# First expert stage of a two-layer graph network: logits and mixture turned in whole 128x128 blocks, VectorE and ScalarE work in another order

## The reference, cut to what matters

```python
gp = softmax(xf @ Wr + br)                    # 4 groups of experts
ep = softmax(einsum('nd,gde->nge', xf, Wgate) + bgate)   # 4 experts in each
# of each softmax the best two are kept (ties: lower index first), the second
# only if both together are <= 0.9; then they are normalised to sum 1
tw = w_group[:, :, None] * w_exp * 0.5        # 16 weights for each row
for e in range(16):
    h = silu(xf @ W1[e]) * (xf @ W3[e])       # 512 -> 32
    out = out + tw[:, e:e+1] * (h @ W2[e])    # 32 -> 512
```

## Time and profile before

| | |
|---|---|
| median of 3 runs | 2476.98 us (2475.22 to 2479.04) |
| profiled execution, its own time | 2480.19 us |
| its span in the profile | 2478.5 us |
| PE busy | 2322.9 us (94%) |
| PE weight loads busy | 1847.2 us (75%) |
| VectorE busy | 1789.8 us (72%) |
| ScalarE busy | 1140.3 us (46%) |
| GpSimd busy | 688.3 us (28%) |
| granted TensorE clock, mean | 0.968 of full |

### The profile page before, as it was taken

One profiled execution on the slowest core, in us unless ns is written; L12 is line 12 of the kernel. 1 busy time (PEld: TensorE's weight loads), 2 busy tenths in 40 slices (PEclk: granted clock), 3 DMA queues, 4 the chain that ended last, 5 costly groups with the idle time before them and its releaser, 6 DMA issues. The chain is left out here.

```text
span 2478.5 us, 33401 instructions
## 1 busy us (share of the span) xinstructions
PE 2322.9 (94%) x10767; PEld 1847.2 (75%) x10770; DVE 1789.8 (72%) x4234; ACT 1140.3 (46%) x2096; POOL 688.3 (28%) x624
## 2 busy tenths in 40 slices
PE   6799886999999999999898999999999699999998
PEld 4577665777777777777677878888877577777776
DVE  7587796787877777777565765555556688888886
ACT  6564322435354545454452222222234776766652
POOL 6465023222222212120131221221222533433420
PEclk9899987999999999999999999999999899999999
DMA  5111133121212122220273344333346656656631
GB/s 167 54 52 52 18 128 99 55 98 60 94 65 90 69 85 73 81 83 33 82 232 99 128 138 135 130 130 130 129 139 201 153 138 179 155 150 179 153 102 52
DMA packets 155873, 271.89 MB, mean 110 GB/s; under 512 B 35538, under 2 KB 36178, under 8 KB 155478
## 3 DMA queue, kind: packets, MB, share of 16 engines
q1 hardware_dynamic: 123014, 203.00, 24.4%
q0 software_dynamic: 32720, 67.19, 11.5%
HBM read 185.82 MB, written 100.41 MB: 115 GB/s over the span
## 5 line engine op out<-in xcount | busy, mean ns | idle before, releaser
L2388 ACT ACTIVATE conv_h<-conv_h 128x512 f32<-128x512 f32 x79 | 50.0, 633 | 305.6 <-DVE conv_h L2317 256.7
L2865 POOL DMA_INDIRECT next_own<-message,net_slot_d x75 | 123.5, 1646 | 153.6 <-DMA next_own<-own 136.2
L2286 DVE TENSOR_TENSOR conv_yl<-conv_pty,conv_yh 128x512 fp32r<-128x512 f32 x79 | 54.7, 692 | 150.7 <-ACT conv_yh L2378 141.4
L1732 ACT ACTIVATE d_act_out<-d_pa 128x512 f32<-128x512 f32 (+1 forms) x80 | 46.1, 577 | 200.1 <-PE d_pa L69 200.1
L1023 POOL DMA_INDIRECT early_val<-values,net_slot_s x79 | 85.3, 1080 | 189.7 <-DVE d_x L1501 88.5
L67 PE MATMUL d_po<-shared_wq_hi,d_hh 128*128 128x512 f32 x316 | 130.7, 414 | 7.2 <-DVE d_hl L1507 3.1
L67 PE MATMUL conv_p<-conv_w_hi,conv_yh 128*128 128x512 f32 x316 | 132.2, 418 | 1.2 <-DVE conv_yl L2286 1.2
L67 PE MATMUL d_pa<-d_xh,xp_w_hi 128*128 128x512 f32 (+1 forms) x320 | 129.8, 406 | 0.0
L67 PE MATMUL d_pc<-d_xh,shared_wv_hi 128*128 128x512 f32 (+1 forms) x320 | 129.6, 405 | 0.0
L68 PE MATMUL d_pa<-d_xl,xp_w_hi 128*128 128x512 f32 (+1 forms) x320 | 126.7, 396 | 0.0
L69 PE MATMUL d_pa<-d_xh,xp_w_lo 128*128 128x512 f32 (+1 forms) x320 | 126.4, 395 | 0.0
(11 more groups left out here) (618 smaller groups left out, 7190.6 us busy)
## 6 DMA issues: line engine op xcount, KB each, us to landing
conv_yin<-y SPq DMA_DIRECT2D x79, 256.0 KB, 2.7
h<-conv_h SPq DMA_DIRECT2D x79, 256.0 KB, 2.0
own<-xp_own_buf SPq DMA_DIRECT2D x79, 256.0 KB, 2.0
next_own<-own SPq DMA_DIRECT2D x79, 256.0 KB, 4.5
next_x<-y SPq DMA_DIRECT2D x79, 256.0 KB, 3.3
out<-d_res SPq DMA_DIRECT2D x79, 256.0 KB, 2.6
y<-d_y SPq DMA_DIRECT2D x78, 256.0 KB
d_x<-in_x SPq DMA_DIRECT2D x10, 1024.0 KB
```

What stands on the lines that cost most here:

```text
L1732: act_.activation(act_out[:, cc % 2, cols(g)], pa[cc % 2][:, cols(g)], ACT.Tanh, scale=0.5).then_inc(tanh_done, 1)
L2286: v.tensor_tensor(lo[:, t % 2, :], bank[t % 2][:], hi[:, t % 2, :].bitcast(F32), ALU.subtract)\
L2388: act_.activation(h[:, t, :], h[:, t, :], ACT.Relu).then_inc(h_made, 1)
L2865: pool.indirect_dma_start(own[n][:, t, :], None, k.message2[:, :], bass.IndirectOffsetOnAxis(ap=k.slot["d"][:, T * g + t:T * g + t + 1], a ...
```

## The change

The logits' high and low parts now stand in the router's weights twice, in columns 0 to 39 and 64 to 103. Both halves of `ptr` are copied (each 64 partitions x 256 columns) into one tile of 128 x 256, so that tiles 0 and 1 stand above one another, and 2 and 3; two transposes of 128x128 turn them. High and low are now added by VectorE, in one more step of `routing` (26 steps). The mixture is turned in two blocks in the same way: two tiles side by side in `parts`, two transposes, two copies of 64 x 256 into a `mix_t` whose other places stay zero, and the spreading constant is there twice.

The order on VectorE and ScalarE is new: additions 0 and 1 stand before `scale_up(g, 2)`, addition 2 before `low_hidden(g, 2)`, and only addition 3 and the statistics of two tiles before `scale_gate(g, 3)`; the third tile's statistics follow it, and `front1` is now inside `routing`, after step 7 behind `back(g, u, 0)`; `back(g, u, 1)` is after step 9, and `front1_end(g + 2)` after step 15 instead of at the next body's start. ScalarE begins a body with `norm1`, makes `norm0` of tiles 0 and 1 before `split(g, 1)`, and `finish(g - 1, u, 0)` after `tanh(g, 2)`.

```diff
-        fold = c.sb("fold", [2 * SETS * 4, SETS * 4])
...
-        logit_t = c.sb("logit_t", [2 * SETS * 4, GR])
+        logit_t = c.sb("logit_t", [P, 2 * P])
...
-        parts = c.sb("parts", [P, T, P], F32R)
+        parts = c.sb("parts", [P, T, HALF_P], F32R)
...
-        NSTAT, NROUTE = 4, 25
+        NSTAT, NROUTE = 4, 26
+        SET4 = SETS * 4
+        pair_rows = [slice(0, HALF_P), slice(HALF_P, P)]
...
+        def tile_pairs(rows, b):
+            return rows[:].rearrange("p (a b n) -> p a b n", a=2, b=2)[:, :, b, :]
...
             def constants():
-                v.memset(wr[:, :, 2 * SETS * 4:P].bitcast(F32), 0.0).then_inc(router_made, 1)
-                v.tensor_tensor(fold[:], k.ident[0:2 * SETS * 4, 0:SETS * 4],
-                                k.ident[0:2 * SETS * 4, SETS * 4:2 * SETS * 4], ALU.add).then_inc(router_made, 1)
-                v.memset(parts[:, :, 2 * EXPERTS0:P].bitcast(F32), 0.0).then_inc(router_made, 1)
+                for b in range(2):
+                    v.memset(wr[:, :, b * HALF_P + 2 * SET4:(b + 1) * HALF_P].bitcast(F32), 0.0).then_inc(router_made, 1)
+                    v.memset(tile_pairs(mix_t, 1 - b)[pair_rows[b]].bitcast(F32), 0.0).then_inc(router_made, 1)
+                v.tensor_copy(wr[:, :, HALF_P:HALF_P + 2 * SET4], wr[:, :, 0:2 * SET4].bitcast(F32)).then_inc(router_made, 1)
+                v.memset(parts[:, :, 2 * EXPERTS0:HALF_P].bitcast(F32), 0.0).then_inc(router_made, 1)
...
-                link(v.tensor_tensor(prob[:].rearrange("p (t s) e -> p t (s e)", t=T),
-                                     ptr[:, 0:T * SETS * 4].rearrange("p (t n) -> p t n", t=T),
-                                     rbias[:].unsqueeze(1).broadcast_to([P, T, SETS * 4]), ALU.add))
+                flat = prob[:].rearrange("p (t s) e -> p t (s e)", t=T)
+                turned_ = ptr[:, 0:T * HALF_P].rearrange("p (t n) -> p t n", t=T)
+                link(v.tensor_tensor(flat, turned_[:, :, 0:SET4], rbias[:].unsqueeze(1).broadcast_to([P, T, SET4]), ALU.add))
+                link(v.tensor_tensor(flat, turned_[:, :, SET4:2 * SET4], flat, ALU.add))
...
             def body(i, c_):                      # VectorE
                 if behind:
                     back_mean(i, c_ - 1)
-                if mid:
-                    front1_end(g + 1)
...
-                chunk(g, 1)
+                scale_up(g, 1)
                 if mid:
                     low(g + 1, n1, 2)
...
                 if front:
                     front0_end(g + 2)
+                scale_gate(g, 1)
                 low_hidden(g, 1)
                 if behind:
                     back_end(g - 1)
+                if front:
+                    add(g + 2, u2, 0)
+                    add(g + 2, u2, 1)
                 scale_up(g, 2)
...
                 scale_gate(g, 2)
+                if front:
+                    add(g + 2, u2, 2)
                 low_hidden(g, 2)
                 scale_up(g, 3)
                 if front:
-                    for t in range(tiles(g + 2)):
-                        add(g + 2, u2, t)
-                    front1_begin(i, c_ + 2)
+                    if tiles(g + 2) == T:
+                        add(g + 2, u2, 3)
+                    front1_begin(i, c_ + 2, 0)
+                    front1_begin(i, c_ + 2, 1)
                 scale_gate(g, 3)
+                if front and tiles(g + 2) == T:
+                    front1_begin(i, c_ + 2, 2)
                 low_hidden(g, 3)
                 if mid:
-                    routing(g + 1, {6: lambda: back(g, u, 0), 10: lambda: back(g, u, 1)})
+                    def first_back():
+                        back(g, u, 0)
+                        if front:
+                            front1(i, c_ + 2)
+                    between = {7: first_back, 9: lambda: back(g, u, 1)}
                     if front:
-                        front1(i, c_ + 2)
+                        between[15] = lambda: front1_end(g + 2)
+                    routing(g + 1, between)
                     back(g, u, 2)
                     back(g, u, 3)
...
             def logits_copy(g):
-                act_.activation(logit_t[:], ptr[0:2 * SETS * 4, :], ACT.Copy).then_inc(logits_out, 1)
+                for b in range(2):
+                    act_.activation(logit_t[pair_rows[b]].rearrange("p (a n) -> p a n", a=2), tile_pairs(ptr, b)[pair_rows[b]],
+                                    ACT.Copy).then_inc(logits_out, 1)
...
             def mix_copy(g):
-                act_.activation(mix_t[:], ptr[:], ACT.Copy).then_inc(mix_out, 1)
+                for b in range(2):
+                    act_.activation(tile_pairs(mix_t, b)[pair_rows[b]], ptr[pair_rows[b], 0:2 * P].rearrange("p (a n) -> p a n", a=2),
+                                    ACT.Copy).then_inc(mix_out, 1)
...
             def body(i, c_):                      # ScalarE
+                if mid:
+                    norm1(g + 1, u1)
                 tanh(g, 0)
                 mix_copy(g)
-                if mid:
-                    norm1(g + 1, u1)
...
-                split(g, 1)
-                if behind:
-                    finish(g - 1, u, 0)
                 if front:
                     norm0(g + 2, u2, 0)
                     norm0(g + 2, u2, 1)
+                split(g, 1)
                 tanh(g, 2)
+                if behind:
+                    finish(g - 1, u, 0)
...
             def turn_logits(g):                   # PE
-                pe.wait_ge(logits_out, g + 1)
-                for t in range(T):
-                    last = pe.matmul(ptr[:, t * SETS * 4:(t + 1) * SETS * 4], logit_t[:, t * P:t * P + P],
-                                     fold[:], start=True, stop=True)
+                pe.wait_ge(logits_out, 2 * g + 2)
+                for a_ in range(2):
+                    last = pe.transpose(ptr[:, a_ * P:a_ * P + P], logit_t[:, a_ * P:a_ * P + P], k.ident[:])
                 last.then_inc(logits_turned, 1)
...
             def turn_mix(g):
-                for t in range(T):
-                    last = pe.transpose(ptr[:, t * P:t * P + P], parts[:, t, :].bitcast(F32), k.ident[:])
+                for a_ in range(2):
+                    last = pe.transpose(ptr[:, a_ * P:a_ * P + P],
+                                        parts[:, 2 * a_:2 * a_ + 2, :].rearrange("p t n -> p (t n)").bitcast(F32), k.ident[:])
                 last.then_inc(mix_turned, 1)
```

More of the change, by code:

```diff
@@ L1455, in front0_end, with front1_begin @@
                 v.tensor_tensor(shift[0][:], shift[0][:], rs[0][:], ALU.mult).then_inc(shift_made[0], 1)
-            def front1_begin(i, c_):
+            def front1_begin(i, c_, t):
                 g = i * XS + c_
[L1459 to L1464, removed]
+                if t == 0:
+                    v.wait_ge(x1_made, 4 * g + tiles(g) + 4)
+                    if in_range(i, c_, -1):
+                        v.wait_ge(x1_normed, 4 * g)
+                    hold(v)
+                v.bn_stats(st[1][:, t, :], x[c_ % XS][:, t, :])
             def front1(i, c_):
-                statistics(v, i * XS + c_, c_ % XS, 1, 2)
+                g = i * XS + c_
+                statistics(v, g, c_ % XS, 1, tiles(g) - 1)
             def front1_end(g):
@@ L1697, in _ @@
             v.tensor_tensor(expert_r[:], expert[:], expert2[:], ALU.add).then_inc(expert_made, 1)
-            front1_begin(0, 1)
+            v.wait_ge(expert_made, 1)
+            v.tensor_copy(expert_r[HALF_P:HALF_P + 2 * EXPERTS0], expert_r[0:2 * EXPERTS0].bitcast(F32)).then_inc(expert_made, 1)
+            for t in range(T - 1):
+                front1_begin(0, 1, t)
             v.wait_ge(routed_in, 16)
@@ L1701, in _ @@
             front1(0, 1)
+            front1_end(1)
             bodies(v, body)
@@ L1741, in logits_copy @@
                 act_.wait_ge(logits_done, g + 1)
-                act_.activation(logit_t[:], ptr[0:2 * SETS * 4, :], ACT.Copy).then_inc(logits_out, 1)
+                for b in range(2):
+                    act_.activation(logit_t[pair_rows[b]].rearrange("p (a n) -> p a n", a=2), tile_pairs(ptr, b)[pair_rows[b]],
+                                    ACT.Copy).then_inc(logits_out, 1)
             def softmax_exp(g):
-                act_.wait_ge(route, NROUTE * g + 3)
+                act_.wait_ge(route, NROUTE * g + 4)
                 act_.activation(prob[:], prob[:], ACT.Exp).then_inc(exp_done, 1)
@@ L1840, in _ @@
             pe.sem_inc(mix_turned, 1)
-            pe.wait_ge(router_made, 3)
+            pe.wait_ge(router_made, 6)
             def turn(g, t, first=False):
@@ L1848, in turn @@
                 elif not first:
-                    pe.wait_ge(mix_out, g)
+                    pe.wait_ge(mix_out, 2 * g)
                 for kc in range(KC):
@@ L1908, in body @@
                     turn_mix(0)
-                    pe.wait_ge(expert_made, 1)
-                    pe.wait_ge(mix_out, 1)
+                    pe.wait_ge(expert_made, 2)
+                    pe.wait_ge(mix_out, 2)
```

(2 more changed lines are left out.)

## The result

| | before | after |
|---|---|---|
| median of 4 runs each | 2478.01 us (2475.22 to 2480.59) | 2434.52 us (2430.37 to 2435.73) |
| ratio, 95% interval | | 0.9821 [0.9809, 0.9834] |
| profiled execution, its own time | 2480.19 us | 2430.37 us |
| first `turn` to last product of `down`, in the profile | 817.2 us | 771.5 us |
| one body, mean of 17 | 40.78 us | 38.30 us |

The account below looks back on a forecast made before the run. TensorE (PE), 99% busy, was taken to bound the kernel: 18.2 + 4.4 + 7.3 + 7.9 = 37.8 us, less about 3.6 us, is 34 us off the 2477.0 us median, so 2443 us; range 2435 to 2453 us.

Parts of the forecast that it names:

- (a): PE's `turn_logits`: two transposes replace eight small fp32 products, saving 0.96 us a body, 18.2 us in 19 bodies.
- (b): PE's `turn_mix`: two transposes instead of four, saving 0.22 us, 20 times, 4.4 us.
- (c): PE's gap in `down` before tile 0's fourth hidden block goes: 0.43 us, 17 times, 7.3 us.
- (d): PE's gap in `down` before tile 2: 0.53 us, 15 times, 7.9 us; 0.2 us of it taken as left.
- A matmul of 512 columns takes 0.235 us of PE, from start to start: PE's step between products, read from the kernel before and used to time the new body's requests.
- an earlier tanh: ScalarE's moved work lets VectorE's fourth-block gate start 0.25 us after the body's last spread product starts, instead of 0.65.
- The additions' waits hold nothing new: VectorE's earlier additions: claimed no new waiting, since the rows to be added were asked for a body earlier.
- Rival D: Fourth block's gate not earlier, tanh 1.8 us later; larger gaps eat the turns' savings: 2477 us, no change; chance 0.03.
- Rival E: ScalarE's `split(g, 1)` behind `norm0` waits for GpSimd's power, delaying tanh and `scale_up(g, 3)`: slower, 2499 us; chance 0.04.
- B: Rival: gap before tile 2 stays whole, VectorE as late as before; 2447 us, up to 2450; chance 0.20.
- C: Rival: waits keep their size elsewhere (tile 3 or mixture), only the turns' 22.6 us left: 2454 us; chance 0.08.

Follow-up runs that it names:

- e1: Kernel after plus an unused tile in `fold`'s place, so the stage's tiles behind it stand 96 bytes further on; 34.8 us faster than the kernel before.
- h_new_again: The kernel after, unchanged, measured once more on another chip: 2435.73 us, 39.7 us under the kernel before there.
- f1: Kernel after with the first expert stage's tiles 32 bytes further on, by an unused tile: 2437.96 us, ratio 0.9866 to the kernel before.
- f2: Kernel after with the first expert stage's tiles 64 bytes further on, by an unused tile: 2430.71 us, ratio 0.9838 to the kernel before.
- e3: Kernel before with only the new turns, copies and routing step, old order of VectorE and ScalarE, old places with the long step: 2479.18 us against 2479.98.
- e2: Kernel before with `fold` allocated last in the stage, so its tiles stand 96 bytes lower, no instruction changed: 7 us faster.
- f3: Kernel after with 32 unused bytes ahead of the graph convolution's weights and again ahead of its activations: 2423.04 us, ratio 0.9803 to the kernel before.
- f4: Kernel after with 32 unused bytes ahead of the graph convolution's activations alone: 2422.98 us, ratio 0.9803 to the kernel before.
- g1: Kernel after with unused tiles in all stages to shift the operands' distances: 8.7 us faster than the kernel after, ratio 0.9804 to the kernel before.
- e4: Kernel before with only the new order of VectorE and ScalarE, old turns, `fold` in its place: 0.95 us a body faster.

## Why the prediction was off

The range ended at 2435 us, and the measurement is 2434.52, with the forecast at 2443. Point by point, with e1 as the kernel in which only the forecast's own parts work. e1 and the kernel after were measured on different chips, so their times alone part them poorly (ratio 0.9839 to 0.9875 for e1, 0.9821 to 0.9848 for `h_new_again`); f1 and f2, side by side, and the profiles' stages part them clearly.

- (a) `turn_logits`: foreseen 0.96 us a body. Spread and turn together took 0.325 + 0.998 us before and 0.231 + 0.135 after: 0.96. Right. Two transposes take 0.14 us from start to start, and one lasts 0.27 us in the profile. The Trainium skill (TensorE: Matmul & The Clock Gate, Part 4: PE-mode transpose) gives about 275 ns for a bf16 one; these fp32 ones agree with that in length, and their share of PE is a quarter of it, as argued from the earlier trace rows.
- (b) `turn_mix`: foreseen 0.22 us; 0.354 to 0.135: 0.22. Right.
- (c), (d): foreseen 0.43 + 0.53 less 0.2 for what is left, 0.76 us; `down` went from 12.25 to 11.43 us in e1: 0.83. Right, a shade low.
- Together 1.94 us a body foreseen, 2.06 in e1. In time: 34 us foreseen, 34.8 measured for e1 and, by f1 (other places with the long step), 2471.74 - 2437.96 = 33.8. The stage alone, though, is 37.7 us shorter in e1's profile: 0.12 us more in each of 18 bodies are 2.2 of the 3.7 that this lies above the forecast, the rest stays open. By the stages the forecast was thus 3.7 us low in its own parts, and 8.0 us low in the next point.
- The step that failed is the one that looked safest: "A matmul of 512 columns takes 0.235 us of PE, from start to start" was read from the kernel before and carried over to the new one. It became 0.229. 96 products with W1 and W3 in each body at 0.0042 us less make 0.40 us; the eight blocks of them took 22.80 us in e1 and 22.44 after, 0.36. In `down` the shorter step yields only 0.05 us, not 48 x 0.005 = 0.25: there VectorE's `back` sets the end, and PE waits longer instead (10.9 us in all against 7.9 in e1). From e1 to the kernel after the stage is 8.0 us shorter (779.5 to 771.5), from f1 to f2 the time 7.2 us. That is the missing part, within what the kernel's two measurements differ by (39.7 and 43.5 us of gain).
- ScalarE's order was credited with an earlier tanh, hence with the gate at 0.25 instead of 0.65: 0.4 us a body. Taking it back puts the gate at 1.01 and costs 10.4 us, and not through tanh but through the additions that wait for `norm0`; "The additions' waits hold nothing new" looked at the rows to be added alone, and not at the rows that they are added to. This didn't move the forecast, as the order was part of it.
- Rival D (the turns' gain is eaten by larger gaps if the gate isn't earlier) is what e3 is: 2479.18 against 2479.98 us. It was right as a mechanism. Rival E didn't come: VectorE waits 0.82 us for PE ahead of the gate, not for tanh. B and C didn't come either, with 0.24 us of waits a body.

The removed line of `fold` stood in the diff, and I counted it as an instruction and not as 96 bytes ahead of everything else. The mean step of 0.233 to 0.234 was in the trace of the kernel before in several stages, and one of 0.2296 to 0.2309 too (the products with `ex_w2t` and `ex_w` in the last): that there were two sorts of steps could have been seen.

## What to carry to other kernels

When an edit adds or drops a tile, everything allocated behind it moves: compare the start-to-start step of products that the edit doesn't touch before crediting the edit, and use an unused tile of the same size as control. If PE bounds a stage, try a few small unused tiles between the weights and the activations; here 32 bytes in one stage were worth some 6 us of 2430. And price a removed instruction by what is waited for behind it: the turns alone were worth nothing, the order alone 0.95 us a body, both 2.06.

## What the runs showed of the hardware that was not expected

- The mean step from one 512-column product to the next comes in two sorts at the full granted clock, about 0.229 and 0.234 us, 2% apart. The difference of the operands' starts modulo 256 bytes goes with it: short at 0 and 64, long at 32, 96, 160, 192 and 224, and nearly so (0.2326) at 128. It was switched on and off by moved or unused tiles in e1, e2, f1, f2, f3, f4 and g1.
- Even in the kernel after, the first steps of `down` are long ones: in `h_new_again` the six from 805.48 to 806.87 are 0.232 each, the 15 behind 807.09 are 0.227, so 0.229 is their mean. At 64 (W3 in f2) there is no such settling; they stay at 0.229 on average. Why there are two sorts at all stays open; no other relation than the modulo-256 one was tried by design, and 128 was met in one stage only.
- The first layer's stretch differs by up to 9 us between executions of kernels that have the same instructions and places there (last `qkv_pp` product at 296.0 us in f3, 305.1 in e4). Comparing stages, not whole spans, takes this out.
